# Two hidden-state load buffers against four in the down projection of an S4 + AWQ feed-forward layer on eight cores

## What is computed

```python
def reference(...):
    x = L0_attn_u
    xn = _layernorm(x, axis=-1)
    x = x + attn(xn, ...) + ffn(xn, ...)
    return x

def ffn(x, ...):                       # D = 4096, I = 11008
    x2 = x.reshape(-1, x.shape[-1])
    w_gate = _dequantize(gate_qweight, gate_scales, gate_qzeros)   # (q - z) * s
    w_up = _dequantize(up_qweight, up_scales, up_qzeros)
    h = silu(x2 @ w_gate) * (x2 @ w_up)
    w_down = _dequantize(down_qweight, down_scales, down_qzeros)
    return (h @ w_down).reshape(...)
```

## Time and profile before

| | us |
|---|---|
| median of the 2 runs shown (9461.4 and 10094.83) | 9778.12 |
| the profiled execution | 9555.47 |
| its span on the slowest core (core 4) | 9553.9 |
| fastest core of it (core 1) | 9426.4 |
| stage B on core 4, first to last matmul | 6136.6 to 9533 |

### The profile page before, as it was taken

How to read it: one execution, slowest core, us unless ns; L and a number is a source line. 1 busy time by engine, 2 the same in 40 slices (tenths; PEclk the granted TensorE clock), 3 DMA queues, 4 the chain that set the end, 5 groups by cost and what they waited for, 6 DMA issues and landing times.

```text
span 9553.9 us, 88844 instructions; the slowest of 8 cores (9426.4 to 9553.9 us)
## 1 busy us (share of the span) xinstructions
PE 7878.2 (82%) x35185; PEld 3557.5 (37%) x35892; DVE 2731.7 (29%) x5716; ACT 632.8 (7%) x874; POOL 276.9 (3%) x516
## 2 busy tenths in 40 slices
PE   1148889999999999999999999585866859585868
PEld 0123334444444444444444444232322324232323
DVE  4210023333333333333333333313133131313131
ACT  0541100000000000000000000000000000000000
POOL 0200000000000000000000000000000000000000
PEclk9998889999999999999999999797988979798877
DMA  1311144344334334334434433446556564656453
GB/s 41 105 66 53 53 104 102 90 96 101 89 96 102 89 95 103 90 95 102 91 93 103 92 92 88 167 170 214 180 201 209 179 216 164 209 174 220 167 190 133
DMA packets 1179352, 1199.92 MB, mean 126 GB/s; under 512 B 854906, under 2 KB 903430, under 8 KB 1110854
## 3 DMA queue, kind: packets, MB, share of 16 engines
q1 hardware_dynamic: 945978, 731.65, 26.2%
q10 hardware_dynamic: 198144, 360.80, 13.5%
q0 software_dynamic: 34816, 101.74, 3.1%
HBM read 1077.43 MB, written 116.56 MB: 125 GB/s over the span
## 4 chain that ended last, share of the span: by engine, by line
PE 79%; DMA 10%; DVE 4%; ACT 4%; issue 1%; SPq 1%; DVEq 0%; ACTq 0%; POOL 0%; POOLq 0%
PE pg L800 25%; PE pu L812 25%; PE pd L1008 24%; PE pcv L644 5%; DMA hbl<-hscr 4%; DMA rpz<-zsc_d 4%; DVE wd_slab L947 1%; DVE s_tb L944 1%; ACT s_xnT L619 1%; DVE s_nib L938 1%; ACT s_xnb L591 1%; PE ptr_ps L607 1%; ACT s_cv L658 1%; ACT L658 0%; ACT L619 0%
## 5 line engine op out<-in xcount | busy, mean ns | idle before, releaser
L1008 PE MATMUL pd<-wd_slab,hbl 128*128 128x512 bf16 x10788 | 2546.8, 398 | 962.5 <-DMA hbl<-hscr 640.5
L800 PE MATMUL pg<-s_xnT,wg 128*128 128x512 bf16 x10789 | 2380.1, 379 | 53.3 <-DVE wg L772 41.6
L812 PE MATMUL pu<-s_xnT,wu 128*128 128x512 bf16 x10786 | 2377.6, 379 | 11.7
L1008 PEld LDWEIGHTS pd<-wd_slab,hbl 128*128 128x128 bf16 x11008 | 1112.5, 102 | 2396.8 <-issue 1382.2
L800 PEld LDWEIGHTS pg<-s_xnT,wg 128*128 128x128 bf16 x11008 | 1076.0, 98 | 1343.8 <-issue 45.0
L812 PEld LDWEIGHTS pu<-s_xnT,wu 128*128 128x128 bf16 x11008 | 1078.8, 98 | 1297.1
L763 DVE TENSOR_SCALAR s_nib<-ig 128x256 int16<-128x256 int16 x1376 | 237.7, 279 | 2605.9 <-DMA rep_zg<-zsc_g 1884.8
L1030 DVE TENSOR_SCALAR xnc<-xcb,s_rstd,s_nbias 128x512 f32<-128x512 f32 x128 | 69.9, 546 | 1911.6 <-PE pd L1008 1791.2
L644 PE MATMUL pcv<-s_T,s_xnT 128*128 128x512 bf16 (+3 forms) x2258 | 507.8, 387 | 110.7 <-ACT s_cv L658 107.3
L834 DVE TENSOR_TENSOR hb<-hb,pu 128x2048 bf16<-128x2048 bf16 x86 | 196.7, 2288 | 939.9 <-PE pu L812 939.9
L826 ACT ACT_TABLE_LOAD x86 | 110.3, 1283 | 4495.6 <-PE pg L800 4495.6
(11 more groups left out here) (123 smaller groups left out, 1311.9 us busy)
## 6 DMA issues: line engine op xcount, KB each, us to landing
hbl<-hscr SPq DMA_DIRECT2D x320, 1024.0 KB, 5.3
rep_sg<-ssc_g ACTq DMA_DIRECT2D x344, 256.0 KB, 5.1
rep_zg<-zsc_g ACTq DMA_DIRECT2D x344, 256.0 KB, 6.0
rep_su<-ssc_u ACTq DMA_DIRECT2D x344, 256.0 KB, 5.5
rep_zu<-zsc_u ACTq DMA_DIRECT2D x344, 256.0 KB, 6.2
rps<-ssc_d SPq DMA_DIRECT2D x80, 1024.0 KB, 7.5
rpz<-zsc_d SPq DMA_DIRECT2D x80, 1024.0 KB, 9.8
hscr<-hb SPq DMA_DIRECT2D x86, 512.0 KB, 3.4
```

Source lines behind the costliest of these rows:

```text
L800: mm = tensor.matmul(out=pg[:, 512 * c:512 * (c + 1)], lhsT=wg[t % 2][:, 128 * K:128 * (K + 1)], rhs=s_xnT[:, MROWS * K + 512 * c: MROWS * ...
L812: mm = tensor.matmul(out=pu[:, 512 * c:512 * (c + 1)], lhsT=wu[t % 2][:, 128 * K:128 * (K + 1)], rhs=s_xnT[:, MROWS * K + 512 * c: MROWS * ...
L1008: mm = tensor.matmul(out=pd[pbase + jj][:], lhsT=hbl[hB % 2][:, 512 * (i - i0h) + 128 * jj: 512 * (i - i0h) + 128 * (jj + 1)], rhs=wd_slab ...
```

## The change

Four buffers `hbl` take the place of two. Block hB goes into `hbl[hB % 4]`, each buffer with a semaphore of its own; inside a quad the load of block hB waits for block hB - 4. At a quad's start blocks 0, 1, 2 and 3 wait for blocks 8, 9, 10 and 7 of the quad before (the last block that used the same buffer). To pay for the 16 KB per partition, `s_tb2` (8 KB) goes: the subtraction writes its bf16 result over its own int16 input, through a bitcast of `s_nib2`.

```diff
-        s_tb2 = sbB("s_tb2", [128, BW * 512], BF16)
         HBW = 8
-        hbl = [sbB(f"hbl{b}", [128, HBW * 512], BF16) for b in range(2)]
+        NHBUF = 4
+        hbl = [sbB(f"hbl{b}", [128, HBW * 512], BF16) for b in range(NHBUF)]
...
-                CV.inc(vector.tensor_tensor(out=s_tb2[:, 0:bw * 512], in0=s_nib2[:, 0:bw * 512],
+                tb2 = s_nib2[:].bitcast(BF16)
+                CV.inc(vector.tensor_tensor(out=tb2[:, 0:bw * 512], in0=s_nib2[:, 0:bw * 512],
                                             in1=rpz[b % 2][:, 0:bw * 512], op=ALU.subtract))
...
-                                            in0=s_tb2[:, 0:bw * 512],
+                                            in0=tb2[:, 0:bw * 512],
...
-                    if hB >= 2:
-                        sync.wait_ge(CT.h, td2[(e, quad, HBW * (hB - 2) + min(HBW, NNT - HBW * (hB - 2)) - 1)])
+                    if hB >= NHBUF:
+                        pb2 = HBW * (hB - NHBUF)
+                        sync.wait_ge(CT.h, td2[(e, quad, pb2 + min(HBW, NNT - pb2) - 1)])
                     else:
                         qk = (e, quad - 1) if quad >= 1 else (e - 1, 3)
-                        prev_b = NHB - 1 if (NHB - 1) % 2 == hB % 2 else NHB - 2
+                        prev_b = NHB - 1 - ((NHB - 1 - hB) % NHBUF)
+                        if prev_b > NHB - 1 - NHBUF:
+                            pass
+                        prev_b = max(b for b in range(NB + NHB) if b < NHB and b % NHBUF == hB % NHBUF)
...
-                    HLp[hB % 2].inc(sync.dma_start(
-                        out=hbl[hB % 2][:, 0:hw * 512].rearrange("p (I m) -> p I m", m=512),
+                    HLp[hB % NHBUF].inc(sync.dma_start(
+                        out=hbl[hB % NHBUF][:, 0:hw * 512].rearrange("p (I m) -> p I m", m=512),
...
-                    tensor.wait_ge(HLp[hB % 2].h, hl2[(e, quad, hB)])
+                    tensor.wait_ge(HLp[hB % NHBUF].h, hl2[(e, quad, hB)])
```

More of the change, by code:

```diff
@@ L989, in _ @@
                             sync.wait_ge(CT.h, td2[(qk[0], qk[1], last_i)])
-                    HLp[hB % 2].inc(sync.dma_start(
-                        out=hbl[hB % 2][:, 0:hw * 512].rearrange("p (I m) -> p I m", m=512),
+                    HLp[hB % NHBUF].inc(sync.dma_start(
+                        out=hbl[hB % NHBUF][:, 0:hw * 512].rearrange("p (I m) -> p I m", m=512),
                         in_=hscr[quad, :, i0h:i0h + hw, :]), 16)
-                    hl2[(e, quad, hB)] = HLp[hB % 2].n
+                    hl2[(e, quad, hB)] = HLp[hB % NHBUF].n
                 @block.tensor
                 def _(tensor):
-                    tensor.wait_ge(HLp[hB % 2].h, hl2[(e, quad, hB)])
+                    tensor.wait_ge(HLp[hB % NHBUF].h, hl2[(e, quad, hB)])
                     for i in range(i0h, i0h + hw):
@@ L1008, in _ @@
                             mm = tensor.matmul(out=pd[pbase + jj][:],
-                                               lhsT=hbl[hB % 2][:, 512 * (i - i0h) + 128 * jj:
-                                                               512 * (i - i0h) + 128 * (jj + 1)],
+                                               lhsT=hbl[hB % NHBUF][:, 512 * (i - i0h) + 128 * jj:
+                                                                    512 * (i - i0h) + 128 * (jj + 1)],
                                                rhs=wd_slab[:, 512 * i:512 * (i + 1)],
```

## The result

Over 12 runs the changed kernel took 9525.91 us in the median (9100.57 to 10581.09), the kernel before, now with 10 runs, 10222.54 us (9461.4 to 10946.85). The ratio is 0.9622, 95% interval 0.9463 to 0.9782. In most executions of either kernel one die or both spend part of the time at a granted clock near 0.81, and the ratio leaves these executions out. The profiled execution took 9153.92 us (9555.47 before). The forecast was 9208 us, a ratio of 0.964; the median of 9525.91 lies outside the stated range of 9060 to 9480, the profiled execution inside it.

What follows compares the result with a forecast made beforehand. TensorE's work plus its idle time bounds the kernel, 947.9 us of it idle before stage B's matmuls on core 4. Savings of 202 + 53 + 92 = 347 us take 9555.5 to 9208 us, range 9060 to 9480.

Steps and rivals of the forecast that it cites:

- Waits at quad changes and inside quads: Stage B: loads issued further ahead cover their latency, removing 137.4 + 65 = 202 us of TensorE idle time.
- Slow matmuls: First three blocks after each of 24 quad changes: matmuls at the 1.2 GHz level go without the gap, 53 us.
- After the short waits of 1.60 and 0.68 us nothing is lost: Inside quads: matmuls after these waits run at full rate, so nothing more to win there.
- Group changes: Seven group changes: weight loads start two blocks sooner, each gap 74.3 us against 87.47, 92 us in all.
- The start of stage B and the subtraction: Stage B's 112.64 us start wait stays, and the in-place subtraction still takes 2.29 us; no gain from either.
- The sum: Whole kernel: 202 + 53 + 92 = 347 us off 9555.5, giving 9208 us.
- The range: Whole kernel's measured time: 9060 to 9480 us.
- I forecast for an execution like the profiled one: Whole kernel: forecast starts from the profiled 9555.5 us, though the median of two runs shown was 9778.
- 9480 us at 17 further slow quads: Range's upper end: partial cases of a lower TensorE clock in stage B, each slow quad costing 15.7 us.
- The waits or the chain are throughput: Rival, stage B loads: the deeper queue only moves waits; 9273, 9300 or, with both, 9365 us; chance 0.11.
- VectorE slows in place: Rival, subtraction over its own input: runs at half rate; 9293 us, up to 9378; chance 0.03.
- TensorE's clock falls as its gaps close: Rival, stage B: fewer gaps bring granted clock 0.80 to 26 more quads, 9616 us; chance 0.11.

Runs made afterwards that it cites:

- experiment 2: Kernel before, its two hidden-state buffers alternating through all of stage B instead of restarting each quad; core 0's span went from 9439.8 to 9302.9 us.
- experiment 3: Changed kernel with three hidden-state buffers instead of four; spans 9135.6 to 9167.5 us, against 9078.0 to 9095.2 with four on die 0.
- experiment 4: Changed kernel with the next group's weight loads held until block 8 of quad 3 is done; seven group-change gaps sum to 633 us on core 0, against 535.
- experiment 1: Changed kernel with two buffers, leaving only the in-place subtraction; spans 9415.1 to 9471.8 us, against 9426.4 to 9448.8 on die 0 of the kernel before.
- experiment 5: Changed kernel with weight loads of groups 1 to 7 on ScalarE's queue; lowest time 8777.64 us, ratio to the kernel before 0.9306.
- experiment 6: experiment 5 with two hidden-state buffers instead of four; lowest time 9157.79 us, one of two executions.
- experiment 7: experiment 5 with all 11 batches of the next group given to VectorE ahead of quad 3's combine; lowest time 8772.27 us, against 8777.64.
- experiment 8: experiment 5 with quad 3's combine placed between batches 5 and 6 of the next group; lowest time 8742.69 us.
- experiment 9: experiment 8 without loading the zeros of groups 1 to 7 (output wrong); die 0 spans 8529.2 to 8549.4 us in one execution.

## Why the prediction was right and wrong

**Waits at quad changes and inside quads, 202 us: right.** Core 4 lost all 202.7 us. On the other seven cores 185 to 217 us of such waits are gone too, with at most 0.4 us left on any. That the gaps at quad changes were latency and not throughput is shown by experiment 2, where the same two buffers in another order end them. For the short waits it took the deeper queue (experiments 2 and 3).

**Slow matmuls, 53 us: right in kind, undersized.** Core 0, at full clock in both profiles, went from 2463.8 to 2393.8 us of busy time, 70 us. The term was mis-sized in what it left out. The 24 quad changes are worth some 50 us of it, near the forecast 53. The step that failed is "After the short waits of 1.60 and 0.68 us nothing is lost", with "so there is nothing more to win there": it is so for these two waits, but on core 0 six short waits of 2.07 to 2.91 us cost 1.4 to 1.7 us each, 10 us in all. The last 10 us are an estimate from the rows: every run of matmuls ends 0.17 us late (32 in 7.07 us, 192 in 41.60), and 60 runs are gone. Two short waits of core 0, the second with slow matmuls behind it:

```profile
6661.68 53.69 PE L1008 MATMUL pd<-wd_slab,hbl 128*128 128x512 bf16 x248 [2.18 <-DMA hbl<-hscr]
...
6747.03 55.03 PE L1008 MATMUL pd<-wd_slab,hbl 128*128 128x512 bf16 x248 [2.91 <-DMA hbl<-hscr]
```

**Group changes, 92 us: right.** 632.6 to 538.3 us on core 4, 94; over the eight cores 73 to 104, 92 in the mean. That the mean gap is 76.9 us and not 74.3 is because the gaps before had a mean of 90.4, not 87.47. Experiments 3 and 4 show that it is the place of the weight loads: on core 4 a gap is 90 us with two buffers, 83 with three and 77 with four, and one wait gives all of it back.

**The start of stage B and the subtraction, 0: right.** 112.64 against 115.05 us, and experiment 1.

**The sum.** Stage B of core 0 is 3287 us before and 2929 after, 358 us for the forecast 347. Its span fell by 346.6 us, since stage B began 12 us later in that execution. So the close match with 347 is in part luck: the terms on core 0 are 208 (forecast 202), 70 (53) and 80 (92) us, and the late start took 12 off their sum. The slowest core's span fell by 401.5 us, from core 4 to core 7. The rest is clock: core 4 had six slow quads before (6 x 15.7 = 94 us) and some three after (its last group took 47 us longer than the others), and core 7, the slowest after, had none in stage B but began it 43 us later than core 0.

**The range: wrong.** The step that failed is "I forecast for an execution like the profiled one", with the upper end "9480 us at 17 further slow quads". The low clock entered as a rival of the change, at 0.11. It belongs to the executions of both kernels. In the longest execution of the changed kernel, 10581.09 us, die 0 has spans of 9075.3 to 9112.3 at a granted clock of 0.953, and die 1 of 10541.2 to 10579.5 at 0.811. In 9531.32 us, next to the median, die 0 has 9129.3 to 9166.1 and die 1 9466.2 to 9529.8 at 0.91. The kernel before does the same: in an execution of 10645.44 us die 0 has spans of 9450.2 to 9488.1, and die 1 of 10598.0 to 10643.9 at 0.825. So nothing of the change went missing in the median; the slower die was at a lower clock. The two runs shown of before, 6.7% apart, said as much: the sum carried over to both gives 9114 and 9748 us, 9431 in the middle, and a range for the median had to reach 9750. The lower end is off as well, by a sum: 9114 less the 34 us between the terms and their upper bounds (7 + 27) is 9080, not 9060.

**The rivals.** "The waits or the chain are throughput" is false for the change. One step further on, in experiments 5 to 9, the loads of the weights do set the pace. "VectorE slows in place" is false. "TensorE's clock falls as its gaps close" is false as the sole cause: in experiment 9 core 6 was busy for 994 of 1000 us of stage B at clock 1.00, and in experiment 5 core 0 had 0.81 in stage A, where all kernels are the same:

```profile
3000.00:4000.00 1000.00, 1000.00 (x3810) 414.30 (x3809) 279.11 (x723) 45.34 (x29) 0.00 (x0) 0.81 0.34 79
```

The Trainium skill's peak-current limiter (TensorE: Matmul & The Clock Gate, "Seeing it yourself"), 13/16 of full clock for a whole die, agrees in size with this row, and in its unit with the executions above. With this execution its unit and its condition do not agree: in the same stretch of their own spans core 1 had 0.81 as well, but cores 2 to 7 had 1.00, and 2 and 3 are on the same die. In the profiled execution of the kernel before all eight cores were busy for 995 to 1000 us of that stretch, at 1.00. What starts such a stretch stays open. There is no sign that closed gaps make it more frequent: 8 of the 10 executions before and 10 of the 12 after are over 1.5% above the shortest of their kernel. That is too few to rule it out.

## What to carry to other kernels

A load that goes into the buffer of the block just being used costs a full round trip each time, whatever the average bandwidth; look for it where a loop starts anew and its block count doesn't fit the buffers, and try a running index before more memory. In a queue that issues in order, count what stands behind each wait: a quarter of the value of a deeper buffer here (92 of 347 us) was that another operand's loads came forward, and giving them a queue of their own was worth about as much as the deeper buffer (304 against 361 us alone). When a wait only moves as the order changes, as in experiments 7 and 8, leave out part of the loads once to see whether the order is the matter at all.

## What the runs showed of the hardware

- A granted clock near 0.81 comes and goes by die, or on two cores of a die (cores 0 and 1 of experiment 5), in stretches of a millisecond and more, also in code that is equal in all kernels, and moved a span by up to 17% (9075.3 against 10579.5 us in one execution).
- On core 5 of experiment 5, with the DMA engines busy for 0.89 of a stretch at 288 GB/s, a load of 1 MB of scales takes 17.0 us to land in the median, where it took 7.4. The hidden-state loads, on SP's queue, rose from 6.3 to 8.4 us.
- Whether the 1.2 GHz level follows a short wait does not go by the wait's length alone. On core 0 of the kernel before the granted clock is 0.54 in the 3 us behind the wait of 2.91 us and 1.00 behind that of 2.18 us; a wait of 2.07 us is followed by 248 matmuls in 55.37 us, and one of 3.57 us by 192 at the full rate, 41.60 us.
